# Shared late scores, a split last feed-forward chunk, and one evacuation moved to ScalarE, in a fused attention and local-attention kernel

## The chip, the cores and the metric

The kernel runs on one core of a Trainium2 chip. The metric is the device time of one execution in microseconds (us); lower is better. TensorE multiplies matrices into PSUM (8 banks of 128 partitions x 512 fp32 values), VectorE, ScalarE and GpSimd work element by element, and the SyncE queue issues most DMAs. All matmuls here are in fp32.

## The reference

The input is 8 sequences of 512 tokens of width 128. First comes causal attention with 16 heads of width 64 in 8 groups that share keys and values, and a LayerNorm (its position in the kernel is the "a" part). Then come two layers of local attention and a gated feed-forward (the "b" part), and a last LayerNorm.

```
q = einsum('bsd,dhe->bshe', resid, W_Q); k, v likewise with 8 groups
scores = einsum(q, k) / 8;  scores[k > q] = -1e6
z = softmax(scores) @ v;  out = z @ W_out + b_out
...
# twice: x = x + local_attention(rotary(l2norm(h @ wqkv))) @ wo, windows of 64 and the one before
h = layernorm(shift_token(x)) @ w1 + b1;  a, g = split(h)       # 341 columns each
x = x + (a * gelu(g)) @ w2 + b2
```

## The kernel before

A tile is 128 tokens; each sequence has four, i = 0 to 3. The "a" part of tile i needs keys 0 to K, K = 128(i+1). Heads go in pairs: the two heads of a pair lie on partitions 0 to 63 and 64 to 127, and their matmuls use the two row halves of TensorE's array. A unit is 4 pairs for i=0, 2 for i=1, 1 for i=2 and 3 (`PAIRS_OF`), so each tile has 2, 4, 8 or 8 units. For a unit, `scores` (L535) multiplies queries, as the stationary operand of 64 rows and 128 columns, with K keys; VectorE's `maxima` (L898) adds the causal mask, copies to `prob` and takes the extremum; ScalarE exponentiates (L747); GpSimd scales (L1102, L1105); TensorE transposes 64x64 blocks (`turn`, L548); ScalarE and VectorE evacuate one bank each (L754, L910); and `value` (L571) multiplies with v for two pairs at a time, 256 columns per matmul. `project_q` makes two banks per tile; ScalarE evacuates one and VectorE the other into `q_t` (L734, L884). `project_v` is evacuated by VectorE (L889).

The "b" part runs per tile and layer (rotary products, L631, L649, L664, L680 on TensorE), and its feed-forward per group: 15 groups of two tiles and 2 of one, per layer. Its `ffn` makes three chunks of 128 hidden columns (the last has 85 used) for each of the two parts, gate and value, over 256 tokens: `halves` (L496) issues each product of 128 weight columns as two matmuls of 64 weight columns, on the two column halves of the array. ScalarE applies Gelu to the gate part (L843), VectorE's `gate` (L1041) adds the bias to the value part and multiplies.

The order of every engine's work is written out as a string, one letter per step: `SCORE["pe"]` for TensorE has Q, K, V projections, S scores, T transposes, P values, O output product of the "a" part, small letters for the "b" part, and ~ for filling pairs of matmuls near the end. `BANK_DIGITS` gives the PSUM banks that each TensorE step takes. A step that takes a bank first waits for the evacuation of the step that held it (`claim`, `emptied`). Each fp32 matmul of the program appears in the trace as two MATMUL instructions, each with a weight load (LDWEIGHTS, row PEld); a transpose appears as one.

Of the kernel before, what the change touches and what calls it, by code (L numbers as in the profile page):

```python
# [13 lines left out]
P = 128  # L14
# [3 lines left out]
E = 64  # L18
# [68 lines left out]
def summer(l, n):  # L87
# [8 lines left out]
    "act": {"Q": "a_q", "K": "a_k", "E": "a_exp", "T": "a_turn", "V": "a_value", "h": "b_h", "s": "b_square_q", "q":  # L96
            "b_square_k", "v": "b_v", "t": "b_turn_qk", "e": "b_exp", "u": "b_turn_p", "a": "b_value", "r": "b_turn_f", "g":
            "b_gelu", "c": "b_scale"},
    "dve": {"T": "tables", "Q": "a_q", "V": "a_v", "M": "a_max", "I": "a_inverse", "U": "a_turn", "Y": "a_y", "h": "b_h", "t":
            "b_turn_k", "u": "b_turn_q", "l": "b_length_k", "e": "b_length_q", "r": "b_turn_qk", "m": "b_max", "i": "b_inverse",  # L100
# [19 lines left out]
    "act": (  # L120
        "QKQKEEEEEKKQEKTTEEVVEETEEVTTQEEhTEEEVsEVVqvTTTEEEEKVhETEtEEEEsqTTVTTeEEEEEVVeEKQvTTTtEEuEEEaEhVeeTqTTEEsEuEEEaQvVTTT"
        "EEtEVVQEEeKrEheggqgTsEvhTVVtEEETeEEqsQeVvhuTVTTEVVaEEEsEvqhKuTvtTEEhEEEaeeqVKTtTTEEEEEVsQeTTVerEEEsuqgVagKgtEEeehTvT"
        "EETEEsEEtqVvhuTTeEaEEEsQeqVvTuhTTatEEEEsKEVVqeveQtuETrEaggguTheesqtarEgggevVVtheTuEaEEsEqvVQehTTTEEuEEeEVVvqaTsVhEEE"
        "KtTuTEEEKeeasEqVvhrTTTEtEEEgggEEqQTVesTrVtTEEEEuegVaggveEhTeTEEEstEqVEhvuKTTeEEaeqQEsvEVhuTTTtEEEEQEaqVEVseveKTutrah"
        "EEgggeTsvqutreVagVggEETehVtuseaqQEEvTTTheueEEqVVsEEVaKEEvhTtuTTEEEEEEesKaeVqhvTrTTtEEEEEEegggQseVTqVTrTEEEEvgtgguKaV"
        "EeEhTeETEEsvEtqhuTTeVEEQEsaqeEhVvTutTTEEEaEQEEsVVeqevKutrTaggghEuesqeTatvrEEgggeVVtuTheEsEEVqavQeehTTuTEEEasEVVqEVEK"
        "TTEvhtTEEuEEEesaKevqVThrTtTEEEEEgggeEseVQqVTTTturEEEEgggvKaVeehTEEuEEEsvtqETVhTTEaEsEvQEqVuhTTeTetEKEEvEVeVsQaqerEut"
        "TEEagggEuheestaqTrvgggEEVVtTheueqsEEaVveeQTThTEEEEusVVVaqvEEKThuTTEEEtEaEEseeKqvVrThTTEEEtEgggsEQEVqVeTreTTEEEuEgtvg"
        "gKVaEEeeThtTEEEEsuvqhTVeeETEEasvEqQVuhtTTTEEEQvEqaesVVeKrtuEEEaTggghEeqvusetarTgggeEVVhtTEEuevQaqsEeehTTTVEEEEuVEEsq"
        "VVvaKhTTTutEEEEEsaeeKEvTqVhTrtEEEETEEgggseQqVVeTTTtrEEEuVgggEEEaKtehTveEEEsvqhuVETeaTTEEEEesqvhVtTQTTuEEEasEVeVvQqer"  # L130
        "utTEEhKagggEeqTEtuersavgggeVtheuEEEsVQaeEqTvTTehVTEuEEEEEsVVVhvqaTTuTEEtEEEaEqesvheTrVtTTEEEEgggEEsVqVeTrtTueTEEEggg"
        "EVaeehETEtvuETEesvhqaeETTvVEEhEEEsVutTTTqVaVeequrstahvgggetuesqaregggvutehaeehuqsausvvrqtggagrgggetheregggqusehctqua"
        "vsaeetceuevarcugaggrgggrggg"),
    "dve": (
        "QMMQMMMMIVVTQITUIMUMVVMIMMMIUYIQUUMMMMhMIUMItuIleYUUMMMMIMMIUhrUMMMIMUItIuUUUmMMlMMMemIQIMIYiUMMUrMMnMIMmhUIImtwUiMU"
        "UMMlnMMIeMIIuQwUUUMMMrsIMMMmVYmUhIMMVtgglgueIiQAVhUMrMMMmIItUmYIlQuhinUUUMMMethMIMMYIulwnUMrMMMmmIIIVUthweUMMrUMUMMI"
        "IMsmeUUmiuQliMMMItInlMguerggYmmAwIhUMUMUMMrIMIMtulhnUmMiIeMMMmUtQIIuwnUhMUMriMeswMMIlUtmmMIluYQrneiMMmmUwggghInVsUtV"
        "ruliMeMmgggmIAwVAdhrUMnimmtIMuIlQYhwUUMMMMMnIeItiUMslMMhuIIYwUUrnMMMMmmIUetVuIwlhUMMrMsIMUMmmUMiIgtggeUUlIQAuMMrMMMn"
        "ImdUMggIigemAwhYUUiMMMIMItrulhnmeIMMUmUtMMQlIiuwInhUMMrMMUUsIMMetImmluQYwUnriIMMhewmmgggnstAuVdUMMeiIrlgggmUVwAmhVrM"
        "ntMIummYIQilwUUhMMeMMUMtnIilMsIueYwIhUrMMnMMMIMmUmIVUItuwhiUMMUrsMMIMMmUItmegIgQgulAUUMMMMUMIliMndrgggemIAmYhwUUMIMM"  # L140
        "MtIruhlnUmMMMUIeIMtimuwQIhUinUrMMMUMMeMIsltmmQuYIwInrelMUimmwgghgUnVstMVuirAlMeMmwmgggdArInVhMMUItiumlmIYQwhnUUiMMMM"
        "sUetIMIuMeIwlYMMUUhrnMMMMIUmmIIVetuwiUhMMrlMMMsUmUMgIggmtIIAuQUUUrMnMMMMmdIIggigeMmlAYwhUUMMIMnirtIMulIhmmMMMeUUMtIQ"
        "IulwhUnUUMMMMMreisIMmmtQIuYweinlrMMUmmwggghVInIsrVAtuelMiUMmgggVwmAdhrMUtMnemiIImQuYwUUhUiMMMMMMlnstuIIleYIwUhnMMMMM"
        "rMUIUImmtIVwulUhMMMMsUIMeUMruiIgtQggmmIAUUMMMiMMUlnrdIgIggMemmYAhwIUMMrMUMntImuiIhlUmMeUMMtIMQuwIlnhrUUiMMMMMMtUsmQl"
        "emIIuwernMYmimMwUhgggnVtslAVurUIMMmeigggVmwIAdhrMIMUntmmiuIQlYwhUMUiMeMMnIUMMItsIeluYwhnUUrMMMMUMMIImmuteUVwIhUrMMMM"
        "lMMUsIImgIggmtiuQlAUUUrMMMMeIdnMgggYIMmmiArhIwUUMMMtMIiuhnlmmUUMIMMMwIetIQuhrUUlnMiMMMmseIUMtuImeQwMYnrUiMhMmlmgggwI"
        "tVnUsrMVAilVmIumgggewMArUhdMinMmmIutQIYlUUhwMMMMeUMiMnIIshItuleYUUnwMMMMMrMtImmUhIwIUulVriMMMMUsIeMMgggIUmtmuIAUMMrU"
        "nlMeMmiMmgggIdMUAIYihUwMrMIUnmImthMueMlUUMMMIMhIonIwiurtUsUUlommewtYinrleuhmwomggnrsgtmimeluAogggnrAwhmimtwhinlesnwu"
        "otusrlggogewmmgggrsAAdmihmtggglnuAoihertnlmmuwowerimsmndiwnsgwggAsgggdAdgggAd"),
# [111 lines left out]
def program(nc, t_in, out):  # L261
    ctx = ExitStack()
    with ctx:
        def sb(name, shape, dt=F32):
            return ctx.enter_context(nc.sbuf_tensor(name, shape, dt))
# [159 lines left out]
        def banks_of(name, *args):  # L425
            return [psum[:, k, :] for k in BANK_OF[name, args]]
# [834 lines left out]
```

## Time and profile before

| | before |
|---|---|
| median of 3 runs | 1151.34 us (1151.09 to 1151.92) |
| the profiled execution | 1151.44 us, its span 1149.6 us |
| TensorE busy | 1132.4 us, 98% |
| VectorE, ScalarE, GpSimd busy | 1040.9, 1001.2, 958.5 us |
| mean granted TensorE clock | 0.998 |

The span runs from the first to the last instruction of the profiled execution. Busy time is the union of an engine's instructions; matmuls are pipelined and their ends are modelled, so starts are read rather than ends. The chain of work that ended last goes back from the last instruction to what released it, or to the one before it on its engine.

### The profile page before, as it was taken

To read this page: it belongs to the slowest core of one execution; us is meant where nothing else is said; L and a number is where in the kernel's file an instruction comes from. 1 tells how busy PE (TensorE), PEld (TensorE's weight loads), DVE (VectorE), ACT (ScalarE), POOL (GpSimd) and SP (SyncE) were. 2 spreads that over 40 slices of the span, in tenths; PEclk is the share of its full clock that TensorE was granted. 3 is DMA by queue.
4 is the path that set the end of the run, shared out by engine and by line. 5 is a ranking of instruction groups with operands and counts; after the bars stand their busy time and mean duration, and the time that the engine had idled before them with its cause. 6 is when DMAs were issued, how large, how long until landed. Compare 5 with 4: busy or idle time off the path is not lost.

```text
span 1149.6 us, 45236 instructions
## 1 busy us (share of the span) xinstructions
PE 1132.4 (98%) x17504; PEld 820.2 (71%) x17504; DVE 1040.9 (91%) x4019; ACT 1001.2 (87%) x3168; POOL 958.5 (83%) x950
## 2 busy tenths in 40 slices
PE   9999999999999999999999999999999999999987
PEld 7677666777678676777676776777767777666765
DVE  7898899999999899999989899998998989999984
ACT  6888889888899889889898998989888898997795
POOL 2787888889888898888978889888978898988855
PEclk9999999999999999999999999999999999999999
DMA  6001010000110100111001101001001010011010
GB/s 233 11 12 33 16 32 22 21 16 9 31 27 5 45 14 3 41 25 39 14 3 36 38 23 32 17 4 42 9 23 26 4 28 23 14 35 29 11 33 27
DMA packets 31094, 31.85 MB, mean 28 GB/s; under 512 B 12576, under 2 KB 21408, under 8 KB 30752
## 3 DMA queue, kind: packets, MB, share of 16 engines
q1 hardware_dynamic: 30448, 28.17, 9.3%
q8 instruction: 140, 2.29, 0.9%
q10 hardware_dynamic: 432, 0.79, 0.2%
q14 instruction: 74, 0.61, 0.2%
HBM read 10.07 MB, written 2.10 MB: 11 GB/s over the span
## 4 chain that ended last, share of the span: by engine, by line
PE 83%; DVE 6%; POOL 5%; issue 2%; ACT 2%; DMA 0%; SPq 0%; POOLq 0%; DVEq 0%; ACTq 0%
PE psum L496 39%; PE psum L535 11%; PE psum L571 11%; PE psum L548 7%; PE psum L649 5%; PE psum L680 4%; PE psum L631 2%; PE psum L664 2%; DVE prob L898 1%; POOL x_hat L1164 1%; POOL rnorm L1135 1%; PE psum L594 1%; DVE b_prob L980 1%; ACT b_prob L803 1%; POOL b_prob L1152 1%
## 5 line engine op out<-in xcount | busy, mean ns | idle before, releaser
L747 ACT ACTIVATE prob<-prob,negmax 128x512 f32<-128x512 f32 (+3 forms) x512 | 282.7, 558 | 16.1 <-DVE negmax L898 15.3
L898 DVE CUSTOM_DVE_ANT_0 prob<-psum,causal 128x512 f32<-128x512 f32 (+3 forms) x512 | 224.0, 484 | 11.5 <-PE psum L535 9.6
L1102 POOL TENSOR_SCALAR prob<-prob,rowinv 128x384 f32<-128x384 f32 (+1 forms) x256 | 161.2, 649 | 50.1 <-DVE rowinv L904 48.7
L803 ACT ACTIVATE b_prob<-b_prob,b_negmax 128x128 f32<-128x128 f32 x512 | 199.0, 395 | 0.8 <-DVE b_negmax L980 0.7
L496 PE MATMUL psum<-wqkv,h_t 128*64 128x512 f32 x768 | 190.8, 599 | 0.1
L535 PE MATMUL psum<-k_t,q_t 64*128 64x384 f32 (+3 forms) x1024 | 163.5, 443 | 0.7 <-DVE prob_t L910 0.6
L1122 POOL TENSOR_TENSOR r<-r 128x512 f32<-128x512 f32 x120 | 153.4, 1284 | 7.0 <-DVE r L938 6.9
L571 PE MATMUL psum<-prob_t,v 128*64 128x256 f32 x1280 | 153.1, 380 | 0.0
L980 DVE CUSTOM_DVE_ANT_0 b_prob<-psum,band,rnorm 128x128 f32<-128x128 f32 x512 | 145.8, 344 | 5.4 <-PE psum L649 4.9
L1152 POOL TENSOR_TENSOR b_prob<-b_prob,b_rowinv 128x1024 f32<-128x1024 f32 x61 | 116.0, 1902 | 27.7 <-DVE b_rowinv L1000 27.6
L1105 POOL TENSOR_TENSOR prob<-prob,rowinv 128x512 f32<-128x512 f32 x96 | 98.1, 1047 | 36.4 <-DVE rowinv L904 36.3
L571 PEld LDWEIGHTS psum<-prob_t,v 128*64 128x64 f32 x1280 | 89.3, 137 | 54.4 <-issue 16.7
L1139 POOL TENSOR_TENSOR rnorm<-length,minus_half 128x8 f32<-128x8 f32 x64 | 106.6, 1666 | 14.7 <-DVE length L995 14.5
L910 DVE COPY prob_t<-psum 128x512 f32<-128x512 f32 (+1 forms) x176 | 108.5, 633 | 7.0 <-PE psum L548 5.6
L1135 POOL TENSOR_TENSOR rnorm<-length,minus_half 128x8 f32<-128x8 f32 x64 | 106.6, 1666 | 9.4 <-DVE length L988 9.4
L754 ACT COPY prob_t<-psum 128x512 f32<-128x512 f32 (+1 forms) x176 | 92.2, 548 | 22.0 <-PE psum L548 20.8
L548 PEld LDWEIGHTS psum<-ident,prob 64*128 64x128 f32 x2560 | 91.4, 139 | 18.7 <-issue 12.4
L548 PE MATMUL psum<-ident,prob 64*128 64x64 f32 x2560 | 102.2, 224 | 0.5 <-POOL prob L1105 0.5
L747 ACT ACTIVATION_READ_ACCUMULATOR prob<-prob,negmax 128x1 f32 x512 | 99.2, 194 | 0.0
L803 ACT ACTIVATION_READ_ACCUMULATOR b_prob<-b_prob,b_negmax 128x1 f32 x512 | 99.0, 193 | 0.0
L535 PEld LDWEIGHTS psum<-k_t,q_t 64*128 64x128 f32 x1024 | 82.9, 188 | 21.6 <-issue 10.4
L496 PE MATMUL psum<-f_t,w 128*64 128x256 f32 (+1 forms) x816 | 92.7, 369 | 0.9 <-ACT f_t L834 0.9
(104 smaller groups left out, 2725.6 us busy)
## 6 DMA issues: line engine op xcount, KB each, us to landing
vb_mid<-vb SPq DMA_DIRECT2D x112, 128.0 KB, 2.4
x_t<-in_x_t SPq DMA_DIRECT2D x8, 256.0 KB, 3.9
x_n<-in_x SPq DMA_DIRECT2D x8, 256.0 KB, 3.1
x<-x SPq DMA_DIRECT2D x64, 31.8 KB
out<-x SPq DMA_DIRECT2D x15, 128.0 KB, 1.8
wqkv<-in_wqkv SPq DMA_DIRECT2D x1, 1536.0 KB, 11.3
w<-in_w SPq DMA_DIRECT2D x1, 768.0 KB, 13.1
x<-x SPq DMA_DIRECT2D x48, 0.2 KB
```

What stands on the lines that cost most here:

```text
L496: last = mm(out[half(w)], weights[:, half(w)], moving, start=start, stop=stop)
L535: last = mm(banks[h][:, p * K:(p + 1) * K], q_t[half(h), (NT * b + i) % 2, c + p, :], k_t[half(h), b % 2, (c + p) // 2, 0:K], start=True, ...
L548: last = transpose(banks[q][:, o:o + E], prob[half(q), k % PROBS, h, j * P:(j + 1) * P], ident[half(q), half(q)])
L571: last = mm(bank[half(h), p * P:(p + 2) * P], v[:, (NT * b + j) % V_RING, g * E:(g + 1) * E], two_pairs(k % PROB_TS, np_, i, h, p, j), sta ...
L747: last = af(pr, pr, ACT.Exp, bias=negmax[:, k % 4, o:o + 1], scale=-1.0, accum_out=rowsum[:, k % 4, o:o + 1])
L803: last = af(pr, pr, ACT.Exp, bias=b_negmax[:, a, o:o + 1], scale=-1.0, accum_out=b_rowsum[:, a, o:o + 1])
L898: vec.tensor_tensor_reduce(prob[:, k % PROBS, h, p * K:(p + 1) * K], bank[:, p * K:(p + 1) * K], causal[:, S - K:S], -E ** -0.5, 3.0e38, A ...
L980: vec.tensor_tensor_reduce(b_prob[:, a, s, c, :], bank[:, c * P:(c + 1) * P], band[:, min(n % NT, 2 - n % 2), :], rnorm[:, a, 0, 2 * c + s ...
L1102: last = gp.tensor_scalar(pr, pr, rowinv[:, k % 4, h:h + 1], 1.0, ALU.mult, ALU.mult)
L1122: return gp.tensor_tensor(r1[:, a, s, :, :], r1[:, a, s, :, :], r2[:, s, :, :], ALU.add)
L1135: gp.tensor_tensor(rnorm[:, PLACE[l, n] % 2, 0, :], length[:, 0, :], minus_half[:], ALU.pow).then_inc(rnorm_q, 1)
L1152: gp.tensor_tensor(pr, pr, b_rowinv[:, a, :].unsqueeze(2).broadcast_to([P, HB, P]), ALU.mult).then_inc(b_prob_ready, 1)
```

## The change

For the tiles i=0 and i=1 (`JOINT`), the last 64 keys of a tile are masked for its first 64 queries. The new `scores` computes them only for the later 64 queries of each head, for two pairs of heads at once: `q_late` holds, side by side, the late queries of an even pair and of the odd pair after it. Two pairs now take three matmuls on each row half: the even pair with K-64 keys, both pairs' late queries with the last 64 keys, and the odd pair with K-64 keys in reversed blocks of 64. So that the late scores of the even pair fall on partitions 0 to 63, its queries are projected with their halves swapped. The mask gets a second, swapped form; ScalarE and VectorE each copy 256 columns more per projection of such a tile; `value` goes pair by pair, since the halves are to be swapped back for the even ones.

The last feed-forward chunk has 85 columns per part. Now 21 of the value part lie behind the gate part in one product (from column `REST` = 96), and the other 64 are computed by two matmuls that share the 64 weight columns and take half of the tokens each. VectorE's `gate` does that chunk in three pieces. The evacuation of v moves to ScalarE. The strings of order of all five queues and the banks are written anew; in the ones for TensorE, stretches such as TTSS became TSTS. Left out below are the strings, and the host's packing of w1 and b1.

```diff
+REST = 96
+JOINT = (0, 1)
...
-WARM = (3, 2, 2, 4, 2, 4, 3, 2, 1, 9, 2, )
+WARM = (2, 1, 1, 3, 4, 3, 3, 3, 2, 1, 5, 1, 4, )
...
-        causal = sb("causal", [P, S], BF16)
+        causal = sb("causal", [P, 2, S], BF16)
+        q_late = sb("q_late", [P, len(JOINT), CA // 2, P])
...
+        def even_at(i, p):
+            return p // 2 * 3 * E + E if i == 0 else 0
+        def odd_at(i, p):
+            return p // 2 * 3 * E if i == 0 else 4 * E
+        def late_of(bank):
+            return bank.rearrange("p (d x n) -> p d x n", d=2, n=E)[:, :, ::3, :]
...
+                tokens = x_t[:, b % 2, i * P:(i + 1) * P]
+                turned_tokens = tokens.rearrange("p (q n) -> p q n", q=2)[:, ::-1, :]
                 for c in range(4):
-                    last = halves(bank[:, c * P:(c + 1) * P], wq[:, 4 * h + c, :], x_t[:, b % 2, i * P:(i + 1) * P])
+                    moving = turned_tokens if i in JOINT and c % 2 == 0 else tokens
+                    last = halves(bank[:, c * P:(c + 1) * P], wq[:, 4 * h + c, :], moving)
...
-                for p in range(np_):
+                queries = q_t[:, (NT * b + i) % 2, :, :]
+                for p in range(0, np_, 2 if i in JOINT else 1):
+                    keys = k_t[:, b % 2, (c + p) // 2, 0:K]
...
+                    early = keys[:, 0:K - E]
                     for h in range(2):
-                        last = mm(banks[h][:, p * K:(p + 1) * K], q_t[half(h), (NT * b + i) % 2, c + p, :],
-                                  k_t[half(h), b % 2, (c + p) // 2, 0:K], start=True, stop=True)
+                        mm(banks[h][:, even_at(i, p):even_at(i, p) + K - E], queries[half(h), c + p, :], early[half(h)], start=True, stop=True)
+                    for h in range(2):
+                        mm(banks[h][:, even_at(i, p) + K - E:even_at(i, p) + K], q_late[half(h), i, (c + p) // 2, :], keys[half(h), K - E:K],
+                           start=True, stop=True)
+                    backward = early.rearrange("p (x n) -> p x n", n=E)[:, ::-1, :]
+                    for h in range(2):
+                        last = mm(banks[h][:, odd_at(i, p):odd_at(i, p) + K - E], queries[half(h), c + p + 1, :], backward[half(h)], start=True, stop=True)
...
-                for p in range(0, max(np_, 2), 2):
+                for p in range(0, max(np_, 2), 1 if i in JOINT else 2):
...
-                for part in (1, 0):
-                    last = halves(bank[:, (1 - part) * z:(2 - part) * z], w1[:, l, part, ch * P:(ch + 1) * P], f_t[:, 0:z])
+                last = halves(bank[:, 0:z], w1[:, l, 1, ch * P:(ch + 1) * P], f_t[:, 0:z])
+                if ch < CH - 1:
+                    last = halves(bank[:, z:2 * z], w1[:, l, 0, ch * P:(ch + 1) * P], f_t[:, 0:z])
+                else:
+                    for w in range(2):
+                        last = mm(bank[half(w), z:z + z // 2], w1[:, l, 0, ch * P:ch * P + E], f_t[:, w * z // 2:(w + 1) * z // 2], start=True, stop=True)
...
+                if i in JOINT:
+                    last = copy(q_late[:, i, 2 * h:2 * h + 2, :].rearrange("p d (x n) -> p d x n", n=E), late_of(bank))
...
+            def project_v(b, i):
+                act.wait_ge(v_done, nth("pe", "a_v", (b, i)))
+                bank, = banks_of("a_v", b, i)
+                copy(v[:, (NT * b + i) % V_RING, :], bank).then_inc(v_ready, 1)
...
+                if i in JOINT:
+                    last = vec.tensor_copy(q_late[:, i, 2 * h:2 * h + 2, :].rearrange("p d (x n) -> p d x n", n=E), late_of(bank))
...
+            def gated(gelu, value, bias):
+                return vec.scalar_tensor_tensor(out=gelu, in0=value, scalar=bias, in1=gelu, op0=ALU.add, op1=ALU.mult)
...
-                vec.scalar_tensor_tensor(out=u_t[0:k, ch, 0:z], in0=bank[0:k, z:2 * z], scalar=b1[0:k, l, 0, ch:ch + 1],
-                                         in1=u_t[0:k, ch, 0:z], op0=ALU.add, op1=ALU.mult).then_inc(u_ready, 1)
+                if ch < CH - 1:
+                    last = gated(u_t[:, ch, 0:z], bank[:, z:2 * z], b1[:, l, 0, ch:ch + 1])
+                else:
+                    for w in range(2):
+                        gated(u_t[0:E, ch, w * z // 2:(w + 1) * z // 2], bank[half(w), z:z + z // 2], b1[half(w), l, 0, ch:ch + 1])
+                    last = gated(u_t[E:k, ch, 0:z], bank[REST:REST + k - E, 0:z], b1[REST:REST + k - E, l, 1, ch:ch + 1])
```

## Rows read from the trace of the kernel before

**Rows 1.** The page: busy time by engine (share of the span) and instructions.
```profile
PE 1132.4 (98%) x17504; PEld 820.2 (71%) x17504; DVE 1040.9 (91%) x4019; ACT 1001.2 (87%) x3168; POOL 958.5 (83%) x950
```

**Rows 2.** Windows: length, busy us by engine, clock, DMA share, GB/s.
```profile
0.00:50.00 50.00, 47.93 (x630) 37.32 (x632) 39.54 (x147) 34.24 (x112) 25.88 (x34) 1.00 0.39 140
50.00:1080.00 1030.00, 1028.26 (x15936) 740.57 (x15934) 950.19 (x3675) 917.22 (x2907) 890.60 (x875) 1.00 0.09 22
1080.00:1149.60 69.60, 56.21 (x948) 42.35 (x944) 51.18 (x199) 49.73 (x151) 42.05 (x43) 0.97 0.10 26
```

**Rows 3.** Waits of TensorE, the longest in total: us, times, longest.
```profile
PE psum L496 <- ACT o_t L825: 1.7, 3, 0.7
```

**Rows 4.** Timeline of TensorE's matmuls, 593 to 601 us: start, us, work.
```profile
593.88 2.76 PE L496 MATMUL psum<-f_t,w 128*64 128x256 f32 x24
596.47 1.03 PE L496 MATMUL psum<-wqkv,h_t 128*64 128x512 f32 x4
597.33 0.28 PE L680 MATMUL psum<-b_prob_t,vb_mid 128*64 128x64 f32 x4
597.44 0.29 PE L680 MATMUL psum<-b_prob_t,vb 128*64 128x64 f32 x4
...
599.55 1.48 PE L496 MATMUL psum<-w,u_t 128*64 128x128 f32 x24
600.86 1.37 PE L496 MATMUL psum<-wout,z_t 128*64 128x128 f32 x22
```

**Rows 5.** The chain that ended last, five stretches: start, us, instructions.
```profile
207.64 0.64 PE psum L664 x16
208.28 0.50 PE psum L548 x16
...
208.85 0.95 PE psum L535 x16
...
506.89 0.92 PE psum L535 x8
...
557.65 0.70 PE psum L535 x4
...
699.23 1.34 PE psum L535 x8
```

**Rows 6.** TensorE's weight loads by form: busy us, mean ns, idle before.
```profile
L548 PEld LDWEIGHTS psum<-ident,prob 64*128 64x128 f32 x2560 | 91.4, 139 | 18.7 <-issue 12.4 <-POOL prob L1102 3.8 <-POOL prob L1105 0.9
L571 PEld LDWEIGHTS psum<-prob_t,v 128*64 128x64 f32 x1280 | 89.3, 137 | 54.4 <-issue 16.7 <-DVE negmax L898 1.5 <-ACT prob_t L754 0.4
L535 PEld LDWEIGHTS psum<-k_t,q_t 64*128 64x128 f32 x1024 | 82.9, 188 | 21.6 <-issue 10.4 <-ACT prob_t L754 3.8 <-DVE negmax L898 0.9
```

**Rows 7.** VectorE by form, as above.
```profile
L938 DVE TENSOR_TENSOR r<-psum,table 128x512 f32<-128x512 f32 x128 | 86.9, 679 | 0.0
L935 DVE TENSOR_TENSOR r<-psum,table 128x512 f32<-128x512 f32 x128 | 86.8, 678 | 3.8 <-PE psum L496 1.7 <-ACT sq L774 1.5 <-issue 0.3
L910 DVE COPY prob_t<-psum 128x384 f32<-128x384 f32 x64 | 34.3, 550 | 2.7 <-PE psum L548 2.1
L889 DVE COPY v<-psum 128x512 f32<-128x512 f32 x32 | 21.6, 679 | 0.2
L1041 DVE SCALAR_TENSOR_TENSOR u_t<-psum,b,u_t 85x256 f32<-85x256 f32 x30 | 14.2, 472 | 1.3 <-ACT u_t L843 1.0
L1041 DVE SCALAR_TENSOR_TENSOR u_t<-psum,b,u_t 128x128 f32<-128x128 f32 x8 | 2.4, 341 | 0.0
```

**Rows 8.** ScalarE by form, as above.
```profile
L761 ACT COPY z_t<-psum 128x256 f32<-128x256 f32 x96 | 35.0, 370 | 21.7 <-PE psum L571 21.6
L734 ACT COPY q_t<-psum 128x512 f32<-128x512 f32 x32 | 18.7, 584 | 4.0 <-PE psum L496 3.9
```

**Rows 9.** The chain near both ends: start, us, what.
```profile
16.72 1.15 DVE v L889 x2
...
1142.88 0.85 DVE u_t L1041 x3
```

More of the change, by code:

```diff
@@ L532, in scores @@
                 banks = claim("a_scores", b, i, c)
-                for p in range(np_):
-                    for h in range(2):
-                        last = mm(banks[h][:, p * K:(p + 1) * K], q_t[half(h), (NT * b + i) % 2, c + p, :],
-                                  k_t[half(h), b % 2, (c + p) // 2, 0:K], start=True, stop=True)
+                queries = q_t[:, (NT * b + i) % 2, :, :]
+                for p in range(0, np_, 2 if i in JOINT else 1):
+                    keys = k_t[:, b % 2, (c + p) // 2, 0:K]
+                    if i not in JOINT:
+                        for h in range(2):
+                            last = mm(banks[h][:, p * K:(p + 1) * K], queries[half(h), c + p, :], keys[half(h)], start=True, stop=True)
+                        continue
+                    early = keys[:, 0:K - E]
+                    for h in range(2):
+                        mm(banks[h][:, even_at(i, p):even_at(i, p) + K - E], queries[half(h), c + p, :], early[half(h)], start=True, stop=True)
[3 more added lines that the diff above has]
+                    backward = early.rearrange("p (x n) -> p x n", n=E)[:, ::-1, :]
+                    for h in range(2):
+                        last = mm(banks[h][:, odd_at(i, p):odd_at(i, p) + K - E], queries[half(h), c + p + 1, :], backward[half(h)], start=True, stop=True)
                 last.then_inc(scored, 1)
@@ L570, in value @@
                             g = 2 * ((c + p) // 2) + h
-                            last = mm(bank[half(h), p * P:(p + 2) * P], v[:, (NT * b + j) % V_RING, g * E:(g + 1) * E],
-                                      two_pairs(k % PROB_TS, np_, i, h, p, j), start=(j == 0), stop=(j == i))
+                            values = v[:, (NT * b + j) % V_RING, g * E:(g + 1) * E]
+                            if i in JOINT:
+                                place, turned_probs = slice(p * P, (p + 1) * P), two_pairs(k % PROB_TS, np_, i, h, p - p % 2, j)[:, p % 2, :, :]
+                                if p % 2 == 0:
+                                    turned_probs = turned_probs[:, ::-1, :]
+                            else:
+                                place, turned_probs = slice(p * P, (p + 2) * P), two_pairs(k % PROB_TS, np_, i, h, p, j)
+                            last = mm(bank[half(h), place], values, turned_probs, start=(j == 0), stop=(j == i))
                 last.then_inc(valued, 1)
@@ L733, in project_q @@
                 bank, = banks_of("a_q", b, i, h)
-                copy(q_t[:, (NT * b + i) % 2, 4 * h:4 * h + 4, :].rearrange("p c n -> p (c n)"), bank).then_inc(q_act, 1)
+                last = copy(q_t[:, (NT * b + i) % 2, 4 * h:4 * h + 4, :].rearrange("p c n -> p (c n)"), bank)
+                if i in JOINT:
+                    last = copy(q_late[:, i, 2 * h:2 * h + 2, :].rearrange("p d (x n) -> p d x n", n=E), late_of(bank))
+                last.then_inc(q_act, 1)
             def project_k(b, i):
@@ L843, in gelu @@
                 af(u_t[0:k, ch, 0:z], bank[0:k, 0:z], ACT.Gelu, bias=b1[0:k, l, 1, ch:ch + 1]).then_inc(gelu_done, 1)
[L845 removed]
+            walk("act", {"a_q": project_q, "a_k": project_k, "a_v": project_v, "a_exp": exponentials, "a_turn": turn, "a_value": value, "b_h": turn_h,
                          "b_square_q": square_q, "b_square_k": square_k, "b_v": value_in, "b_turn_qk": turn_qk, "b_exp": exponentials_b,
@@ L883, in project_q @@
                 bank, = banks_of("a_q", b, i, h)
-                vec.tensor_copy(q_t[:, (NT * b + i) % 2, 4 * h:4 * h + 4, :].rearrange("p c n -> p (c n)"), bank).then_inc(q_dve, 1)
-            def project_v(b, i):
-                dve.wait_ge(v_done, nth("pe", "a_v", (b, i)))
-                bank, = banks_of("a_v", b, i)
-                vec.tensor_copy(v[:, (NT * b + i) % V_RING, :], bank).then_inc(v_ready, 1)
+                last = vec.tensor_copy(q_t[:, (NT * b + i) % 2, 4 * h:4 * h + 4, :].rearrange("p c n -> p (c n)"), bank)
+                if i in JOINT:
+                    last = vec.tensor_copy(q_late[:, i, 2 * h:2 * h + 2, :].rearrange("p d (x n) -> p d x n", n=E), late_of(bank))
+                last.then_inc(q_dve, 1)
             def maxima(b, i, c, h):
@@ L897, in maxima @@
                     o = h * np_ + p
-                    vec.tensor_tensor_reduce(prob[:, k % PROBS, h, p * K:(p + 1) * K], bank[:, p * K:(p + 1) * K], causal[:, S - K:S],
+                    masked, seen, mask = prob[:, k % PROBS, h, p * K:(p + 1) * K], bank[:, p * K:(p + 1) * K], causal[:, 0, S - K:S]
+                    if i in JOINT and p % 2 == 0:
+                        seen, mask = bank[:, even_at(i, p):even_at(i, p) + K], causal[:, 1, S - K:S]
+                    elif i in JOINT:
+                        masked, mask = masked.rearrange("p (x n) -> p x n", n=E), mask.rearrange("p (x n) -> p x n", n=E)
+                        if i == 0:
+                            seen = bank[:, even_at(0, p - 1) - E:even_at(0, p - 1) + K].rearrange("p (x n) -> p x n", n=E)[:, ::2, :]
+                        else:
+                            masked, mask = masked[:, ::-1, :], mask[:, ::-1, :]
+                            seen = bank[:, K - E:2 * K - E].rearrange("p (x n) -> p x n", n=E)
+                    vec.tensor_tensor_reduce(masked, seen, mask,
                                              -E ** -0.5, 3.0e38, ALU.add, ALU.min, negmax[:, k % 4, o:o + 1]).then_inc(max_ready, 1)
@@ L1073, in end_stats @@
                 last.then_inc(var_e_ready, 1)
-            walk("dve", {"tables": tables, "a_q": project_q, "a_v": project_v, "a_max": maxima, "a_inverse": inverse, "a_turn": turn,
+            walk("dve", {"tables": tables, "a_q": project_q, "a_max": maxima, "a_inverse": inverse, "a_turn": turn,
                          "a_y": residual_a, "b_h": turn_h, "b_turn_k": rotate_k, "b_turn_q": rotate_q,
```

150 lines of the change are left out of this document (77 added, 73 removed), and 3 rows, old and new, of the table LETTERS.

## The prediction

> **What bounds the kernel now.** I read the page first. TensorE is busy for 98% of the span; VectorE, ScalarE and GpSimd follow at 91, 87 and 83% [rows 1]. A mean hides stages, so I took three stretches next [rows 2]; the granted clock is 1.00, the 2.4 GHz level, in two of them and 0.97 in the last. From 50 to 1080 us TensorE is busy 1028.26 of 1030 us: there, every nanosecond taken from or added to its queue moves the end. In the last 69.6 us it idles 13.4 us, waiting for chains of the others; in the first 50 it idles 2.1 us. The longest total wait of its matmuls for one releaser is 1.7 us [rows 3]. So: sum TensorE's queue, then look at both ends, then ask whether the others can still keep up.
>
> A sum needs the price of one pass. Every fp32 matmul of the program is two instructions, and two matmuls on different halves of the array run side by side, so four instructions are two passes. From one start to the next in the timeline [rows 4], 12 passes of 256 columns take 596.47 - 593.88 = 2.59 us, 0.216 each; 12 of 128 columns take 600.86 - 599.55 = 1.31, 0.109 each; with 64 columns two passes take 597.44 - 597.33 = 0.11 to 0.12, 0.058 each. All these have 64 weight columns a half.
>
> The scores (L535) have 128 weight columns, and their rows look different. A weight load takes 188 ns there and 137 ns elsewhere [rows 6]: 51 ns for 64 more columns, 0.8 ns a column, thus 102 ns or somewhat more for 128. The chain shows what this does [rows 5]. A run of scores behind transposes has a surcharge: with K=384, 4 instructions take 0.70 us and 8 take 1.34, so two passes take 0.64 and about 0.056 is left over. With K=256, four passes take 0.92 = 4 x 0.216 + 0.056. With K=128, eight take 0.95, less 0.056 makes 0.112 a pass, above the 0.109 of the other kinds. I read: the next weights load while one pass streams; a 128-column load of some 112 ns is just covered by 128 columns, well covered by 256, and not covered by the short pass of a transpose, whence the 0.056. Transposes, which also load 128 columns, show 139 ns: their single-instruction form loads faster, so nothing hides behind them but their own kind.
>
> The Trainium skill (TensorE: Matmul & The Clock Gate, section LDWEIGHTS) says that a weight load's time is its columns over 1.2 a nanosecond. By that, 107 ns for 128 and 53 for 64, and the difference is what the trace shows. Its section on the back-to-back gap gives instead a floor of about 60 cycles for matmuls up to 64 columns, without a weight load; by that rule the new short passes would cost what rival A takes.
>
> **Scores, tile i=0.** A unit had 4 pairs of heads, 8 passes of 128 columns. Now each two pairs have three slots of 64 columns, 12 passes, each with 128 weight columns. If a load takes at least 112 ns, each of the 12 still takes 0.112: streaming halves, and nothing is gained. Four passes more are 4 x 0.112 = 0.45 us; the last is followed by a small load and gives back about 0.05. That is +0.40 us for each of 16 units: **+6.4 us**. Lower bound 0.058 a pass: 12 x 0.058 - 8 x 0.112 = -0.20, -3.2 us over all. Upper bound 0.119 (0.063 for a transpose pass, 8 in 0.50, plus 0.056): +7.7.
>
> **Scores, tile i=1.** A unit had 4 passes of 256, 0.864 us. Now 4 of 192 (0.1625 each, midway between 0.109 and 0.216) and 2 of 64. With 0.112 to 0.119 for the short ones it is 0.874 to 0.888: +0.01 to 0.02 on 32 units, **+0.5 us**. With 0.058 it would be 0.766, -0.10, -3.1 us over all.
>
> **Values of these tiles.** 96 slots of 256 columns become 192 of 128, 64 weight columns each: 4 x 0.109 - 2 x 0.216 = 0.004 us, **+0.4 us**.
>
> **Feed-forward.** In each double group one slot falls from 256 to 128 columns: 2 x (0.216 - 0.109) = 0.214, 30 times; in the four singles 2 x (0.109 - 0.058) = 0.10. Total -6.8 us. Two doubles and the singles lie behind 1080 us, where TensorE has slack, so **-6.0 us** count.
>
> **The order.** I counted letters in the two TensorE lists. Scores (S) that come right behind a transposing or other short step (T, t, h, p, f): 106 before, 155 after, since TTSS gave way to TSTS. Each costs the 0.056 above: 49 x 0.056 = +2.7. Changes between row halves (S T h t s p f) and column halves (the rest): 274 before, 280 after. One costs 0.14: 16 transposes take 0.64 us as L664 behind a projection and 0.50 as L548 behind other transposes [rows 5]. +0.8. Together **+3.5 us**. Warm-up pairs in the tail: 34 to 33, nothing. ScalarE's exchanges of function table: 62 by both lists.
>
> **The others.** VectorE loses 32 copies of v at 0.679 (-21.6), gains 16 copies to q_late of 256 columns (0.679 for 512 and 0.550 for 384, so 0.42 for 256: +6.7), and in each gate of chunk 2 two pieces more: the 85-row one of 256 stays as the rest piece, and two of 128 at 0.34 come on top in 30 groups (+20.4), two of 64 at about 0.27 in four (+2.2) [rows 7]. Net +7.7, to 1048.6. ScalarE gains 32 x 0.584 and 16 x 0.370 = +24.6, to 1025.8 [rows 8]. Reversed blocks cost nothing in the rows (r<-psum with and without a swap, 0.679 and 0.678), so the masks and maxima stay. Both engines have 8% or more in hand, and TensorE's work grows too, which covers them; but fuller queues deliver later, and behind a late evacuation stands the next claim of its bank, with all of TensorE's list behind it. I take **+1 us** (bounds -1.7, all of TensorE's idle there, and +5, what 0.5% of that stretch makes).
>
> **Start.** The chain runs over VectorE from 13.5 to 25.5 us and holds two copies of v, 1.15 us [rows 9]; they go, two q_late copies of 0.42 come: **-0.4 us** (bounds -1.1, +0.5). The mask's 128 KB more travel among the first loads; ident, behind it, is wanted only by the first transposes. Nothing.
>
> **Tail.** The last gate stands in the chain, u_t x3 for 0.85 us, between the feed-forward and the last product [rows 9]. It gets 0.55 longer; the three single groups before it and the two doubles (0.68 each) lie where VectorE is busy 51 of 69.6 us and partly on the path: **+1.5 us** (0.5 to 3.4).
>
> **Sum.** 6.4 + 0.5 + 0.4 - 6.0 + 3.5 + 1.0 - 0.4 + 1.5 = +6.9 us. The profiled execution took 1151.44 (span 1149.6, 1.8 around it), the median is 1151.34; so 1158.3, rounded to 1158.5 us, 0.6% slower.
>
> **Rivals.** *A: only streamed columns count.* A 64-column pass costs 0.058 whatever its weights. Both score terms turn round, from +6.9 to -6.3: 13.2 less, 1145.3 us, faster. For it speaks that 64-column passes do run at 0.058 in L680; against it that these load 64 weight columns, and that the score rows show both 0.112 and the 0.056. It decides as soon as a 128-column load takes under some 70 ns. Chance 0.12.
> *B: the loads bind, but the new lists save elsewhere.* In the tail 13.4 us are idle and the warm-up pairs fill more; if the new order shortens that by 4 to 7 us, the result is 1151.5 to 1154.5. Against it: the last 60 letters of the TensorE list are nearly the same. Chance 0.18, nearly all of it within 0.2% or just above.
> *C: the others become the bound.* If the fuller VectorE and ScalarE queues make TensorE wait 0.5% of the steady stretch and the whole of the tail's gate pieces counts, add 4 + 2: 1164.5. Against: TensorE waits 1.74 us in 1030 now, with VectorE at 92% there. Chance 0.10.
> The forecast itself has 0.60, with 1155 to 1162 as its own range.
>
> **Numbers.** 0.2%, 2.3 us, is about what a measurement of this kernel tells from no change. Below 1149.0: A, and a little of B: 0.13. Up to 1153.6: most of B: 0.15. Above: 0.72. For 8 in 10 I leave out A and half of C: 1149.5 to 1164.
>
> **What would show it.** In the profile after: passes of L535's successor with 64 columns start some 0.11 apart, the K=128 units take about 1.35 us in the chain instead of 0.95, the K=256 ones stay near 0.92 and follow transposes more often; the weight loads still show 188 ns. TensorE stays above 97% busy. The last feed-forward chunk's matmuls show 128 columns at 0.109 a pass; ScalarE near 1026 us busy, VectorE near 1049. If the 64-column score passes start 0.06 apart, I was wrong by rival A; if TensorE idles by more than 5 us between 50 and 1080, by C.

## The result, and the profile after

The changed kernel takes 1160.52 us (median of 4 runs, 1159.12 to 1162.87) against 1151.44 us; the ratio is 1.0081, with a 95% interval of 1.0061 to 1.0100. It is slower by 0.8%. Its runs differ with their mean granted clock: 1159.12 and 1159.38 us at 0.999, 1161.65 at 0.998, 1162.87 at 0.996; "The order" below comes back to this. One of the 11 runs of joint_1 took 1271.01 us at a granted clock of 0.85 and is left out of its interval. The forecast was 1158.5 us, with a range of 1149.5 to 1164. The profiled execution took 1159.38 us, its span 1157.6, 8.0 more than before.

The page after, busy time by engine, beside [rows 1]:

```profile
PE 1135.8 (98%) x18140; PEld 840.4 (73%) x18140; DVE 1056.0 (91%) x4071; ACT 1020.7 (88%) x3216; POOL 956.6 (83%) x950
```

The windows after, beside [rows 2]; the last stretch is 8 us longer:

```profile
0.00:50.00 50.00, 47.35 (x700) 38.87 (x702) 38.34 (x142) 36.22 (x117) 24.94 (x33) 1.00 0.41 143
50.00:1080.00 1030.00, 1026.44 (x16416) 755.87 (x16412) 955.84 (x3696) 929.31 (x2928) 884.54 (x873) 1.00 0.09 22
1080.00:1157.60 77.60, 62.02 (x1032) 45.61 (x1030) 61.83 (x237) 55.14 (x174) 47.08 (x46) 0.98 0.10 26
```

TensorE idles 3.6 us of the 1030, against 1.7: it is still the bound. To see where the 8 us arise, I take the last transpose of the "a" part as a mark. It starts at 1037.4 us in the trace of before and at 1042.1 after:

```profile
L578 PE MATMUL psum<-ident,prob x2560: 216/223/275, 21.4 to 1042.1; 64*128 64x64 f32 x197
```

So 4.7 us arise before the mark, and 3.3 behind it (1157.6 - 1042.1 = 115.5 us, against 112.2).

The chain after, where tile i=0 and the first unit of i=1 of one sequence are scored. L560 is the even pair, L562 the shared late queries, L566 the odd pair:

```profile
209.03 0.50 PE psum L578 x16
209.53 0.06 PE psum L630 x2
209.60 0.22 PE psum L560 x4
209.82 0.22 PE psum L562 x4
210.04 0.22 PE psum L566 x4
210.27 0.22 PE psum L560 x4
210.49 0.22 PE psum L562 x4
210.72 0.22 PE psum L566 x4
210.94 0.50 PE psum L578 x16
...
215.01 0.38 PE psum L560 x4
215.39 0.17 PE psum L562 x4
215.56 0.38 PE psum L566 x4
215.94 1.03 PE psum L685 x32
```

These are the rows that decide. Every slot of tile i=0 streams 64 columns and takes 0.22 us for two passes, 0.112 a pass, the same as the 128 columns took before. A unit went from 0.95 us [rows 5] to 210.94 - 209.60 = 1.34. In tile i=1, 0.38 + 0.17 + 0.38 = 0.93 us stand against 0.92. There the two short passes take 0.17 us together, not 0.22: the first starts at 215.22 us and the second has started by 215.28, for the weights of the first were loaded under the 192-column pass ahead (loads of the two passes start at 215.06 and 215.22), and those of the second did not have to queue behind them. So 0.112 is no fixed price of a short pass with 128 weight columns; it appears where the loads have nothing long to hide under.

```profile
215.22 0.22 PE L562 MATMUL psum<-k_t,q_late 64*128 64x64 f32 x2
```

The loads are as long as they were, for the shared queries too:

```profile
L562 PEld LDWEIGHTS psum<-k_t,q_late x256: 187/188/189, 9.6 to 952.6; 64*128 64x128 f32 x128
```

The new feed-forward matmuls of the last chunk and VectorE's pieces, from the groups by form:

```profile
L743 PE MATMUL psum<-f_t,w 128*64 128x128 f32 x120 | 11.7, 273 | 0.0
L1095 DVE SCALAR_TENSOR_TENSOR u_t<-psum,b,u_t 64x128 f32<-64x128 f32 x60 | 20.7, 345 | 1.0 <-ACT u_t L891 0.5
L1095 DVE SCALAR_TENSOR_TENSOR u_t<-psum,b,u_t 21x256 f32<-21x256 f32 x30 | 14.7, 491 | 0.4
L934 DVE COPY q_late<-psum 128x256 f32<-128x256 f32 x16 | 6.7, 416 | 0.0
```

The 128-column matmuls last 273 ns, as such matmuls do elsewhere (274), so the last chunk's product does stream half. By their own rows the two gate pieces take the 20.4 us that were expected (20.7), and the copies the 6.7.

### The profile page after: what moved, and what is told of

Its sections match the earlier page's. It is cut to its first block, busy times and chain, and to the rows that moved or that the text cites. A ratio compares the mean times of both kernels' runs of the same rounds, so it can differ in the third digit from the quotient of the medians.

```text
span 1157.6 us, 46610 instructions
## 1 busy us (share of the span) xinstructions
PE 1135.8 (98%) x18140; PEld 840.4 (73%) x18140; DVE 1056.0 (91%) x4071; ACT 1020.7 (88%) x3216; POOL 956.6 (83%) x950
## 4 chain that ended last, share of the span: by engine, by line
PE 88%; DVE 7%; ACT 2%; issue 1%; POOL 1%; DMA 0%; POOLq 0%; ACTq 0%; DVEq 0%
PE psum L511 40%; PE psum L608 12%; PE psum L556 9%; PE psum L578 7%; PE psum L685 5%; PE psum L716 5%; PE psum L667 3%; PE psum L700 3%; PE psum L560 2%; PE psum L566 2%; PE psum L562 1%; DVE u_t L1095 1%; DVE b_prob L1036 1%; PE psum L630 1%; DVE prob L954 1%
## 5 line engine op out<-in xcount | busy, mean ns | idle before, releaser
L954 DVE CUSTOM_DVE_ANT_0 prob<-psum,causal 128x128 f32<-128x128 f32 (+3 forms) x448 | 203.3, 494 | 9.2 <-PE psum L566 5.9
L608 PE MATMUL psum<-prob_t,v 128*64 128x256 f32 (+1 forms) x1664 | 153.1, 330 | 0.0
L608 PEld LDWEIGHTS psum<-prob_t,v 128*64 128x64 f32 x1664 | 106.1, 137 | 48.8 <-issue 18.4
L1217 POOL TENSOR_TENSOR b_prob<-b_prob,b_rowinv 128x1024 f32<-128x1024 f32 x61 | 115.7, 1897 | 15.9 <-DVE b_rowinv L1056 15.8
L556 PE MATMUL psum<-k_t,q_t 64*128 64x512 f32 (+1 forms) x512 | 122.8, 563 | 0.0
L578 PEld LDWEIGHTS psum<-ident,prob 64*128 64x128 f32 x2560 | 96.6, 139 | 29.7 <-issue 24.5
L578 PE MATMUL psum<-ident,prob 64*128 64x64 f32 x2560 | 107.2, 224 | 0.5 <-POOL prob L1170 0.3
L991 DVE TENSOR_TENSOR r<-psum,table 128x512 f32<-128x512 f32 x128 | 87.2, 682 | 10.4 <-ACT sq L822 7.5
L994 DVE TENSOR_TENSOR r<-psum,table 128x512 f32<-128x512 f32 x128 | 87.2, 681 | 0.0
```

Source lines behind the costliest of these rows:

```text
L556: last = mm(banks[h][:, p * K:(p + 1) * K], queries[half(h), c + p, :], keys[half(h)], start=True, stop=True)
L578: last = transpose(banks[q][:, o:o + E], prob[half(q), k % PROBS, h, j * P:(j + 1) * P], ident[half(q), half(q)])
L608: last = mm(bank[half(h), place], values, turned_probs, start=(j == 0), stop=(j == i))
L954: vec.tensor_tensor_reduce(masked, seen, mask, -E ** -0.5, 3.0e38, ALU.add, ALU.min, negmax[:, k % 4, o:o + 1]).then_inc(max_ready, 1)
L1217: gp.tensor_tensor(pr, pr, b_rowinv[:, a, :].unsqueeze(2).broadcast_to([P, HB, P]), ALU.mult).then_inc(b_prob_ready, 1)
```

## The experiments

The theory to test: short score passes are held at 0.112 us by a 128-column weight load; the feed-forward split saves on TensorE and gives part back through the gate; the orders cost some 3.5 us. Its rivals: streamed columns set the time, or the orders carry all. Each kernel was timed beside the kernel before on the same chip, whose median was 1151.36 to 1151.44 us; intervals are those of the ratio to it.

**joint_none.** The changed kernel, with the shared scores off.

```diff
-JOINT = (0, 1)
+JOINT = ()
...
```

> The changed kernel with JOINT empty: scores and values of tiles i=0 and i=1 as before, no q_late copies; feed-forward, evacuation of v and all orders as in the changed kernel. Theory (a weight load of 128 columns holds each short score pass at 0.112 us): the three terms 6.4 + 0.5 + 0.4 us fall away, and some 0.5 with the copies, so 1152 to 1154 us against 1160.5. Rival (shorter streams save time on TensorE and the new order eats it): undoing them costs 6 us, 1166.

Measured: 1153.34 us, ratio 1.0017 (1.0009 to 1.0026). As the theory says: the shared scores cost 1160.5 - 1153.3 = 7.2 us, where 7.3 and a little for the copies were expected.

**narrow.** The reverse test, in the kernel before: half the columns, the same loads.

```diff
+                W = K // 2 if i == 0 else K
                 for p in range(np_):
...
-                                  k_t[half(h), b % 2, (c + p) // 2, 0:K], start=True, stop=True)
+                                  k_t[half(h), b % 2, (c + p) // 2, 0:W], start=True, stop=True)
...
+                        seen = bank[:, p * K:p * K + E].unsqueeze(1).broadcast_to([P, 2, E])
```

> The kernel before, where the score matmuls of tile i=0 stream 64 key columns for 128 (128 matmuls, each half as wide), and the maxima read these 64 twice. Left out: the scores with the last 64 keys of tile i=0. Theory: the passes stay 0.112 us apart, since the weight load sets them; at most the last pass of a unit gives 0.05 us, so 1150.5 to 1151.5 us. Rival (streamed columns set the time): 128 passes go from 0.112 to 0.058, -6.9 us, 1144.5.

Measured: 1151.65 us, ratio 1.0000 (0.9991 to 1.0009). Streaming half as much changes nothing that can be measured; the rival's 6.9 us lie far outside. No run changed the weight columns alone: that the load is what holds the passes rests on this run together with the rows above, the 0.058 us of 64-column passes under 64-column loads [rows 4] and the short slot of tile i=1. The chain of this kernel, tile i=0 again, beside the 0.95 of [rows 5]:

```profile
208.73 0.06 PE psum L595 x2
208.79 0.89 PE psum L536 x16
209.69 1.02 PE psum L549 x32
```

0.89 is 7 x 0.112 + 0.058 + 0.056: only the last pass, behind which a small load comes, got shorter.

**joint_0 and joint_1.** One of the tiles alone.

```diff
-JOINT = (0, 1)
+JOINT = (0,)        # joint_0;  (1,) in joint_1
...
```

> The changed kernel with the shared late scores in tiles i=0 only. Theory: of the 7.2 us between JOINT empty (1153.3) and both tiles (1160.5), 6.4 + 0.13 belong to i=0: 1159.5 to 1160.5. Rival (each tile costs alike, for instance by the copies and the extra instructions): 1157.

> The changed kernel with the shared late scores in tiles i=1 only. Theory: 0.5 + 0.27 us on JOINT empty (1153.3): 1153.8 to 1154.8. Rival (streams cut from 256 to 192 columns save 3 us): 1150.5. Rival (each tile costs alike): 1157.

Measured: joint_0 1159.44 us, 1.0068 (1.0055 to 1.0080); joint_1 1153.93 us, 1.0019 (1.0010 to 1.0028). From JOINT empty, tile i=0 costs 6.1 us. Tile i=1 costs 0.6 by the medians, which is not told from nothing, as the intervals of joint_1 and joint_none overlap; the 3 us that its rival saves lie outside. Where 192-column passes cover the loads of their neighbours the shared slot is free, and where all are short it costs a full slot. The copies are alike in both and the extra value matmuls twice as many in i=1, so neither can be the cause.

**ffn12.** The changed kernel with the feed-forward and gate of before.

```diff
-                if ch < CH - 1:
-                    last = halves(bank[:, z:2 * z], w1[:, l, 0, ch * P:(ch + 1) * P], f_t[:, 0:z])
-                else:
...
+                for part in (1, 0):
+                    last = halves(bank[:, (1 - part) * z:(2 - part) * z], w1[:, l, part, ch * P:(ch + 1) * P], f_t[:, 0:z])
...
```

> The changed kernel with the feed-forward of before (12 half-matmuls, one gate piece a chunk). Theory: TensorE gets 6 us more in the steady part, the tail loses the extra gate pieces (1.5 to 3): 1163 to 1165 us against 1160.5. Rival (VectorE's extra pieces, 22.6 us, cost more than TensorE saves): below 1159.

Measured: 1162.03 us, 1.0098 (1.0084 to 1.0112), one below the 1163 to 1165. The split is worth 1.5 us net, and the intervals of this and of the changed kernel (1.0061 to 1.0100) overlap, so its sign alone is not shown by this pair. The traces divide it: the last transpose starts at 1046.8 us here and at 1042.1 in the changed kernel, so 4.7 us are saved before the mark; behind it this one needs 1160.2 - 1046.8 = 113.4 us and the changed one 115.5, so 2.1 are given back.

**order_v.** JOINT empty and the feed-forward of before together: what stays is the orders and the evacuation of v (its diff is the two above).

> The changed kernel with JOINT empty and the feed-forward of before: what is left of the change is the new orders, the banks, the swapped mask's transfer and v evacuated by ScalarE. Theory: 3.5 us for the order (49 more scores behind short steps, 6 more changes between halves) and about 0 to 1 for the rest, so 1154.5 to 1156.5 us against 1151.4. Rival (the order costs nothing, all comes from the scores): 1151.4. Rival (all 9 us are the order): 1160.

Measured: 1156.20 us, 1.0039 (1.0027 to 1.0052). So 4.8 us of the 9.1 come with the orders and the moved evacuation by the medians, inside the expected 1154.5 to 1156.5 and against both rivals. From here to joint_none the split saves 2.9 us by the medians. But the two runs at a granted clock of 0.999 and 1.000 took 1154.61 us, 3.2 above the kernel before, and the three at 0.997 and 0.998 took 1156.20 to 1157.62. The trace is of one of the first two, and its span is 3.1 us longer.

**alternate.** An attempt to price the adjacency by itself, in the kernel before: 30 stretches of TensorE's list, each with its bank digits.

```diff
-    ... TTSS ...
+    ... TSTS ...
```

> The kernel before with 30 stretches TTSS of TensorE's list turned into TSTS, banks carried along: scores right behind a short step go from 106 to 136, nothing else moves. Theory: 30 x 0.056 = +1.7 us, 1153.0. Rival (adjacency costs nothing, only waits count): 1151.4 within 0.5, or less, if the evener order feeds VectorE better.

Measured: 1167.53 us, 1.0139 (1.0125 to 1.0153). Neither the theory nor its rival: 16 us. As I read it, the moved transpose comes about a score's length later, and the engines behind it keep their own orders. Waits for transposes on VectorE, in this kernel (in the trace of before they sum to 5.6 us in 13 cases):

```profile
DVE prob_t L910 <- PE psum L548: 16.5, 28, 1.2
PEld psum L548 <- issue: 20.2, 72, 0.8
```

The second row is the idle time of TensorE's weight loads ahead of transposes, 12.4 us before. The run does not isolate the 0.056.

**none_regroup.** The other way round, in the kernel with JOINT empty: 29 stretches TSTS made TTSS.

```diff
-    ... TSTS ...
+    ... TTSS ...
```

> The kernel with JOINT empty, with 29 stretches TSTS of TensorE's list turned back into TTSS, banks carried along (scores behind short steps 155 to 126). Theory of adjacency alone: -1.6 us on 1153.3, 1151.7. Rival (lists are fitted to one another, and a step moved on one engine meets waits on the others, as TTSS to TSTS cost 16 us where adjacency explained 1.7): 1158 or more.

Measured: 1169.23 us, 1.0153 (1.0139 to 1.0166), 15.9 us above joint_none. The rival holds. Some 30 steps of TensorE moved against fitted lists cost about 16 us in either direction, ten times what adjacency can give. The price of 0.056 us rests on the traces, not on a run.

**ffn11.** The feed-forward split alone, on the orders of before.

```diff
-                for part in (1, 0):
-                    last = halves(bank[:, (1 - part) * z:(2 - part) * z], w1[:, l, part, ch * P:(ch + 1) * P], f_t[:, 0:z])
+                last = halves(bank[:, 0:z], w1[:, l, 1, ch * P:(ch + 1) * P], f_t[:, 0:z])
+                if ch < CH - 1:
+                    last = halves(bank[:, z:2 * z], w1[:, l, 0, ch * P:(ch + 1) * P], f_t[:, 0:z])
+                else:
+                    for w in range(2):
+                        last = mm(bank[half(w), z:z + z // 2], w1[:, l, 0, ch * P:ch * P + E], f_t[:, w * z // 2:(w + 1) * z // 2], start=True, stop=True)
...
```

> The kernel before, with the feed-forward of the change alone (11 half-matmuls, gate in three pieces, host packing), all orders as before. Theory: -6 us of TensorE's work in the steady part; VectorE gets 22.6 us more with v still on it (1063 busy of some 1147, 93%), so a part comes back as waits, and the tail gains 1.5 to 3: 1147 to 1150 us against 1151.4. Rival (VectorE binds): 1152 or more.

Measured: 1159.55 us, 1.0071 (1.0058 to 1.0085): the rival, by far. Whatever TensorE saves of the 6.8 us of the sum, it loses more: from 50 to 1080 us it idles 8.4 us, against 1.7 before. Its waits for gated values in this kernel (weight loads, then matmuls; 3.3 and 0.7 us before):

```profile
PEld psum L497 <- DVE u_t L1044: 14.9, 24, 2.0
PE psum L497 <- DVE u_t L1044: 5.8, 10, 1.8
```

**ffn11_v.** The same with v on ScalarE, at the place in its list where v became ready in the trace of before.

```diff
-    "dve": ... "V" ...
+    "act": ... "W" ...      # a_v
-                vec.tensor_copy(v[:, (NT * b + i) % V_RING, :], bank).then_inc(v_ready, 1)
+                copy(v[:, (NT * b + i) % V_RING, :], bank).then_inc(v_ready, 1)
...
```

> The kernel before with the feed-forward split and v evacuated by ScalarE, put into its list where v became ready in the trace of before; all other orders as before. Theory (the split cost 8 us on the old orders since VectorE, 22.6 us fuller, hands the gated values late): with 21.6 us off VectorE again the waits go, 1147 to 1151. Rival (the wait is for the longer gate itself, three pieces between Gelu and the last product, whatever VectorE's load): 1157 to 1160.

Measured: 1165.01 us, 1.0113 (1.0098 to 1.0129). My theory fell. VectorE is 15 us less busy than in ffn11 (1048.4 against 1063.6), and the wait for the gate is the same:

```profile
PEld psum L497 <- DVE u_t L1044: 15.6, 25, 2.0
```

So it is not VectorE's total load. The gate of a group is 0.68 us longer (two pieces of 0.34), and the product behind it is reached at the same step as before. In the orders of before 3.8 steps of TensorE lie on average between the last feed-forward chunk and that product, in the new ones 4.6 (counted in the lists, filling pairs left out). In joint_none, with the same split on the new orders, the wait is half as long:

```profile
PEld psum L511 <- DVE u_t L1095: 7.5, 14, 1.1
PE psum L511 <- DVE u_t L1095: 3.1, 6, 0.9
```

With the gate in one piece the weight loads waited 3.3 us on the orders of before, and on the new ones, in order_v:

```profile
PEld psum L511 <- DVE u_t L1097: 1.2, 4, 0.4
```

That the extra step is what hides it fits these rows, but no run changed that alone: the new orders differ in much else. The 5.5 us between ffn11 and ffn11_v come with v in ScalarE's old list; where they arise I did not pursue.

**after_tail and none_tail.** The last 6 feed-forward groups keep the old chunk and one gate piece; in the changed kernel, and with JOINT empty.

```diff
+def closing(l, g):
+    return GROUPS.index((l, g)) >= len(GROUPS) - 6
...
-                if ch < CH - 1:
+                if ch < CH - 1 or closing(l, g):
...
+                elif closing(l, g):
+                    last = gated(u_t[0:k, ch, 0:z], bank[0:k, z:2 * z], b1[0:k, l, 2, ch:ch + 1])
...
```

> The changed kernel, whose last 6 feed-forward groups (2 double, 4 single) keep the feed-forward and the single gate piece of before in the last chunk. Theory: the extra gate pieces lie in the chain of the tail, which became 3.3 us longer than before: 2 to 3 us less, 1157.5 to 1158.5 against 1160.5. Rival (the tail is longer for its orders or for what it inherits from the steady part): 1160.5 or more.

> The same in the kernel with JOINT empty, so the feed-forward split, v on ScalarE and the new orders stay, without the shared scores: the candidate to beat both. Theory: 2 to 3 us less than 1153.3: 1150.3 to 1151.3, the same as before (1151.4) or just below. Rival: 1153.3.

Measured: after_tail 1157.90 us, 1.0066 (1.0052 to 1.0079); none_tail 1152.52 us, 1.0011 (1.0002 to 1.0020). Both went the expected way, after_tail within its 1157.5 to 1158.5 and none_tail 1.2 us above its 1150.3 to 1151.3, but each interval overlaps the one that it is compared with, so the medians do not show it. The last transpose of each trace is the firmer reading:

```profile
L583 PE MATMUL psum<-ident,prob x2560: 216/223/275, 22.3 to 1045.3; 64*128 64x64 f32 x197
```

```profile
L583 PE MATMUL psum<-ident,prob x2560: 216/223/275, 21.0 to 1037.3; 64*128 64x64 f32 x197
```

The first is after_tail (span 1159.1, so 113.8 us behind the mark), the second none_tail (1151.2, 113.9); with all gates in pieces it was 115.5 in the changed kernel and in joint_none. So the pieces in the tail cost 1.6 to 1.7 us. No kernel of this study beats the one before; none_tail comes within 0.1% of it.

The mark of after_tail comes 3.2 us later than that of the changed kernel, though the two programs are alike up to the last groups. Its clock was lower near the start. First the changed kernel, then after_tail; the granted clock is the third number from the right:

```profile
24.00:28.00 4.00, 2.81 (x34) 1.91 (x32) 3.90 (x16) 2.25 (x8) 1.97 (x2) 1.00 0.01 4
28.00:32.00 4.00, 4.00 (x76) 3.60 (x72) 2.00 (x12) 3.60 (x13) 1.80 (x3) 1.00 0.00 0
```

```profile
24.00:28.00 4.00, 2.47 (x30) 1.85 (x32) 4.00 (x13) 3.16 (x12) 1.33 (x3) 0.87 0.01 4
28.00:32.00 4.00, 4.00 (x44) 2.68 (x42) 0.81 (x6) 1.05 (x4) 0.98 (x1) 0.71 0.00 0
```

The same transposes start 0.91 us later than in the changed kernel before this stretch (22.35 against 21.44) and 2.55 behind it (31.70 against 29.15), so the drop costs 1.6 us. In between, from 27.0 to 29.5 us, the granted clock is 0.50, the 1.2 GHz level. Three of the nine traces with the new orders have it (after_tail, none_tail, joint_1), and none of the five with the orders of before (alternate and none_regroup counted with the orders that they start from). TensorE idled 0.35 and 1.19 us just ahead of it, but 0.34 and 1.19 in the changed kernel too, where the clock stayed; what decides is not shown. The other runs of after_tail fit: 1157.56 to 1157.90 us at 0.999 and 1.000, against 1161.00 and 1161.66 at 0.998 and 0.997.

## Why the prediction was right

**What bounds it.** Right: TensorE is busy 1026.44 of 1030 us after as well, and the 3.6 us of idle time stay under the 5 that rival C asks for.

**Scores, i=0.** Forecast +6.4 us, and 1.35 us a unit in the chain; the chain shows 1.34, and joint_0 6.1 us, which includes the values and the copies. narrow shows that the streamed columns are not what holds these passes: halving them changes nothing. That it is the load is the reading that the rows leave. By the Trainium skill (TensorE: Matmul & The Clock Gate, section LDWEIGHTS), the 128 columns need 107 ns; the trace agrees with passes 112 ns apart. The floor of about 60 cycles for short matmuls, weight load left out, that the same page of the Trainium skill gives (section Back-to-back issue gap) is not what holds here. An estimate from it is 25 ns an instruction, some 50 ns for the two of a pass, beside the 112 measured.

**Scores, i=1, and the values.** Forecast +0.5 us and a share of 0.4; joint_1 gives 0.6, not told from nothing. In the two traces whose clock did not drop, the changed kernel and joint_none, the spans differ by 5.6 us, where 7.3 and the copies were forecast for both tiles.

**Feed-forward and gate.** TensorE's saving was about right in one pair and too large in the other: the split saves 4.7 us before the mark from ffn12 to the changed kernel, and 1039.6 - 1036.5 = 3.1 from order_v to joint_none, where the sum had -6 and +1 of waits. Two terms were mis-sized. The tail: I took +1.5 us, the traces behind the mark give 2.1 for all the gate pieces (ffn12 against the changed kernel), of a tail that is 3.3 us longer; the rest comes with the orders (order_v: 1152.7 - 1039.6 = 113.1, 0.9 more than before). And the waits in the steady part: I took +1 us, and TensorE's idle time there grew by 1.8, 1.5 of it with the split (ffn12 idles 2.1 us, the changed kernel 3.6). I tied these waits to the load of VectorE and ScalarE; ffn11 and ffn11_v show that the wait for the gate does not follow VectorE's load. Its length between Gelu and the next product is what remains, and, as argued above, how many steps the order leaves to hide it.

**The order.** Forecast 3.5 us less 0.4 for the start; order_v measured 4.8 (3.1 to 6.0 by its interval). The sum fits, and fits best where the clock was 0.999 or more (3.2). What the three runs above hold beyond that has about the size of one or two drops of the clock as in after_tail; they have no trace, so this is not shown. The split into 2.7 for adjacency and 0.8 for changes between halves is read from the traces and was not isolated, since both attempts met waits ten times as large. Of the start, only this can be said: TensorE idles 2.65 us in the first 50 instead of 2.07, so the gain of 0.4 did not appear.

**VectorE's sum.** Forecast 1048.6 us, measured 1056.0. The maxima stayed as I held; all of their line together is busy as long as before, first the kernel before, then the changed one:

```profile
0.00:1149.60 1149.60, 225.59 (x1024) 1.00 0.11 28
0.00:1157.60 1157.60, 225.01 (x1024) 1.00 0.11 28
```

The mis-sized term is the -21.6 for the copies of v. From ffn11 to ffn11_v, where they move to ScalarE, VectorE's busy time falls by 1063.6 - 1048.4 = 15.2 us only, which is 6.4 of the missing 7.4. One instruction begins before the last has ended (two copies of 0.679 us take 1.15 in the chain [rows 9]), so count times mean is more than an engine gets back. ScalarE's forecast erred the same way: 14.9 us for the copies of v in that pair (1001.3 to 1016.2) where I added 18.7, and 1020.7 in all where I had 1025.8. It cost little, since neither is the bound.

**The sum.** Scores and values 7.2, orders and v 4.8, the split -2.9: 9.1 us by the medians, against 6.9. By the runs at a clock of 0.999 or more it is less: 1159.25 us for the changed kernel (the middle of two), 1153.27 for joint_none (the median of five) and 1154.61 for order_v give 6.0, 3.2 and -1.3, together 7.9. There two misses partly cancel: scores and values were forecast at 7.3, and the split at -6.0 + 1.0 + 1.5 = -3.5. So the mechanism was right, and the nearness of the sum owes something to luck.

## What to carry to other kernels

Before cutting a matmul into narrower ones, put the weight load beside the pass. In a run of short fp32 passes here, work that streams less than the next stationary operand needs to load was not saved, and each extra slot cost a full load. With 64 weight columns a half a 64-column pass took 0.058 us and with 128 it took 0.112, so cut along the side that also shrinks the stationary operand, or put the short passes behind long ones. A list that was fitted over all engines prices a change only together with its own order: the split that the sum put at 6.8 us less for TensorE made the kernel 8.1 us slower on the orders of before. And take an engine's saving from a run or from the steps between starts, not from count times mean duration.

## What the runs showed of the hardware that I had not expected

In a run of them, passes of 64 and of 128 columns under 128-column fp32 loads start at the same distance, 0.112 us, and halving the streamed columns of 128 matmuls left the kernel's time at a ratio of 1.0000. Swapping 30 neighbouring pairs of independent steps on one engine, whose list has 1381, cost 16 us (1.4%) in one kernel and as much in another in the opposite direction. Two 64-column passes behind a 192-column one start within 0.06 us of each other under the same 128-column loads. Moving 32 copies of 0.679 us off VectorE took only 15.2 us off its busy time. The granted clock dropped to 0.50 near the start in the traces of three kernels and not in those of six others with the same orders, and one such drop cost 1.6 us.
